# Layer 1 of a four-layer graph network: the message pass also folds weights and makes the node's part of the update; update, norm and layer 2's tables run on by groups

## The chip, the cores and the metric

The kernel runs on one core of a Trainium2 chip. The metric is the device time in microseconds (us), the median of the runs of one kernel. Engines are named as the profile names them: PE (TensorE products, PEld its weight loads), DVE (VectorE), ACT (ScalarE), POOL (GpSimd), SP (SyncE, which here issues DMAs).

## What is computed

A graph of 6250 nodes with 128 features and 106250 edges (self loops included) goes through four layers. Each layer takes `h = relu(layernorm(x))` and adds its result to `x`. Layer 0 is a hypergraph attention, layer 3 two graph attentions. The change lies in layer 1, a message network, and at the beginning of layer 2, a gated edge network:

```python
# layer 1, x is h
msg_in = concatenate([x[row], x[col]], axis=-1)
h = relu(msg_in @ mW1 + mb1)
messages = h @ mW2 + mb2
aggregated = segment_sum(messages, col, num_segments=N)
upd_in = concatenate([x, aggregated], axis=-1)
g = relu(upd_in @ uW1 + ub1)
return relu(g @ uW2 + ub2)
# layer 2, what is a function of the node alone
src_h = feat @ W_src + b_src
dst_h = feat @ W_dst + b_dst
se, de = src_h[edge_src], dst_h[edge_dst]
h = gelu(se @ W1a + de @ W1b + b1)
gate = sigmoid(gelu(se @ Wg1a + de @ Wg1b + bg1) @ Wg2 + bg2)
```

The product with `mW2` is linear, so the kernel sums the edges' `h` first and multiplies per node: `aggregated = (sum of h) @ mW2 + degree * mb2`. Likewise `W_src @ [W1a | Wg1a]` and `W_dst @ [W1b | Wg1b]` are folded on the chip, and layer 2's edges gather ready rows from a table of the source's part, while the target's part stays in SBUF.

## The kernel before

The nodes are 49 blocks of 128; `GROUPS` puts them into 12 groups of four blocks and a last one of one block. The edges, sorted by target, make 232 groups of 4 x 128. A stage that goes over nodes is a loop over `t`, in which `staged(t, s)` gives stage `s` the group `t - s`. Everything is ordered by hand: one instruction list for each of five engines, semaphores between them, and `meet()`, at which all five wait for each other, between stages.

**Layer 1's pass** (`c_po`, `c_ve`, `c_ac`, `c_sp`, `c_pe`, one body per edge group). GpSimd gathers the edges' rows by four indirect DMAs into a ring of eight (L619). PE spreads the values of two target blocks over the edges by one-hot matrices, in three bf16 products (L1258); VectorE adds the gathered rows (L1210), ScalarE takes the relu (L1226), PE sums the edges by target, 129 columns wide so that the last is the degree (`sum_pe`, L981), into one of four PSUM banks (`AGc`), and VectorE adds the two sums to `ACC` (`add_ve`, L966 and L969). SP loads the one-hot matrices.

**The update** (`u_pe`, `u_ac`, `u_ve`) has six stages, for each group: turn the sums in `ACC` (`turn4`, L1717) and copy them out on ScalarE; multiply by `mW2` (`times`, L1730), and on VectorE degree times `mb2` (L2085) plus that product (L2088); turn `H` (the node's h) and that result, and copy both out; multiply by the two halves of `uW1`, add `ub1` (L2094), relu on ScalarE; turn, copy out; multiply by `uW2`, add `ub2` (L2099), relu (L2076), add to `X` (L2101). Each of its PSUM tiles has one bank; of each working tile in SBUF there are two.

**The norm** (`stats_ve`, `stats_po`, `scale_ve`, `norm_ac`) goes in four parts of 13, 12, 12 and 12 blocks: VectorE takes mean and variance (L547, L550, L554), GpSimd the power -1/2 (L566), VectorE the product with the mean (L560), ScalarE writes `H = relu(X * rs - mean * rs)` block by block (L581).

**Layer 2's beginning** (`l2_sp`, `l2_pe`, `l2_ac`, `l2_ve`): SP loads 19 weights (L2127) and spills `X` to DRAM; VectorE clears `ACC`; PE folds the weights (four products); then for each group PE turns `H`, ScalarE copies it out (L2173), PE multiplies by both folded weights of 256 columns, and VectorE adds the biases (L2193, L2195); SP stores the source's part as the table (L2131). At the end SP loads `Wg2` (L2135) and waits for it. After a meeting layer 2's pass begins with its gathers (L619).

## Time and profile before

| | |
|---|---|
| median of 3 runs (lowest, highest) | 11647.88 us (11646.78, 11650.18) |
| profiled execution, span | 11656.4 us |
| PE busy | 7944.2 us (68%) |
| DVE busy | 7999.2 us (69%) |
| ACT busy | 5679.0 us (49%) |
| POOL busy | 7499.3 us (64%) |

These are sums over a span with many stages, so they don't tell what binds one. The stages around the change, in us from the span's start: layer 1's pass 6188.9 to 7354.1, its last additions to 7361.0; the update to 7434.5; the norm to 7460.9; folding of layer 2's weights to 7477.4; its tables to 7526.2; the first gather of layer 2's pass at 7530.2. In the views, "x" is a count, a releaser behind "<-" is what ended the wait ahead of an instruction, and the granted clock is a share of TensorE's full speed (1.00 is 2.4 GHz, 0.50 is 1.2 GHz). A matmul's duration contains time in PE's pipeline, so successive ones overlap; how long a run of products keeps the queue is the distance between starts.

### The profile page before, as it was taken

What the parts mean: (1) busy time and instruction counts of PE and PEld (TensorE: products, weight loads), DVE (VectorE), ACT (ScalarE), POOL (GpSimd) and SP (SyncE); (2) the same over time, 40 slices, a digit from 0 to 9 for tenths busy, and PEclk for the clock granted to TensorE, in tenths of its full rate; (3) what the DMA queues carried; (4) which work ended last, traced back from release to release, by engine and by line L of the source; (5) the groups of instructions that cost most, each with busy time, mean ns of one, the idle gap of its engine ahead of it and who ended that gap; (6) DMA issues with size and microseconds to landing.
All of it is one profiled execution on the core that took longest, in us unless ns stands there. A gap on an engine that the chain in (4) does not pass through costs nothing. (4 is left out here: it accounts for less than half of the span.)

```text
span 11656.4 us, 187371 instructions
## 1 busy us (share of the span) xinstructions
PE 7944.2 (68%) x47022; PEld 5850.1 (50%) x47022; DVE 7999.2 (69%) x33310; ACT 5679.0 (49%) x17077; POOL 7499.3 (64%) x7673
## 2 busy tenths in 40 slices
...
GB/s 17 9 20 51 55 55 55 73 122 120 120 121 65 55 55 55 90 216 214 215 163 116 132 131 131 91 155 154 154 153 107 132 140 137 138 106 137 139 137 114
DMA packets 712781, 1297.42 MB, mean 111 GB/s; under 512 B 196562, under 2 KB 369072, under 8 KB 711216
## 3 DMA queue, kind: packets, MB, share of 16 engines
...
q1 hardware_dynamic: 388992, 615.05, 16.5%
...
## 5 line engine op out<-in xcount | busy, mean ns | idle before, releaser
L619 POOL DMA_INDIRECT WK<-tab,IDX x4640 | 4408.7, 950 | 1833.5 <-issue 1335.3
L1522 POOL DMA_INDIRECT B<-tab,IDX x1856 | 1782.1, 960 | 765.6 <-issue 531.9
L619 POOL DMA_INDIRECT H<-tab,IDX x928 | 880.2, 948 | 577.3 <-DVE H L1327 263.3
L1541 DVE TENSOR_REDUCE WK<-PS 128x4 f32<-128x1024 f32 x928 | 1131.1, 1220 | 127.4 <-PE PS L1667 122.3
L1652 ACT ACTIVATE B<-B 128x33 f32<-128x33 f32 x5568 | 1210.7, 308 | 7.9
L922 PE MATMUL PS<-B 128*128 128x130 f32 (+1 forms) x3712 | 777.5, 374 | 393.4 <-ACT B L895 393.2
L1700 PEld LDWEIGHTS PS<-B,H 128*128 128x128 f32 x3712 | 829.8, 333 | 377.8 <-issue 372.4
L1700 PE MATMUL PS<-B,H 128*128 128x132 f32 x3712 | 893.9, 435 | 177.9 <-DVE ACC L1554 177.9
L1667 PE MATMUL PS<-WK,B 27*128 27x512 bf16 x1856 | 689.7, 481 | 389.6 <-DVE WK L1541 386.0
L922 PEld LDWEIGHTS PS<-B 128*128 128x128 f32 x3712 | 661.7, 268 | 581.5 <-ACT B L895 581.5
L883 ACT ACTIVATE B<-PS,PICK 18x512 bf16<-18x512 f32 x464 | 357.0, 769 | 1139.6 <-PE PS L940 1124.0
L981 PE MATMUL PS<-B,WK 128*128 128x129 f32 x1856 | 439.5, 410 | 612.8 <-ACT B L1018 612.8
L1210 DVE TENSOR_TENSOR WK<-PS,WK 128x512 f32<-128x512 f32 x232 | 160.5, 692 | 850.7 <-DMA WK<-tab,IDX 850.7
L459 POOL DMA_INDIRECT pieces<-WK,B x208 | 357.9, 1721 | 574.9 <-ACT WK L447 304.2
L981 PEld LDWEIGHTS PS<-B,WK 128*128 128x128 f32 x1856 | 371.9, 298 | 674.2 <-ACT B L1018 674.2
L1018 ACT ACTIVATE B<-WK 128x128 f32<-128x128 f32 x1856 | 588.3, 388 | 239.1 <-ACT B L694 96.1
L1226 ACT ACTIVATE WK<-WK 128x512 f32<-128x512 f32 x232 | 146.7, 632 | 1028.1 <-DVE WK L1210 1028.1
L1258 PE MATMUL PS<-B 128*128 x2784 | 310.0, 275 | 491.6 <-DVE WK L1210 482.4
L981 PE MATMUL PS<-B 128*128 128x129 f32 x1856 | 459.8, 425 | 257.2 <-ACT B L1018 256.9
L895 ACT ACTIVATE B<-WK 128x128 f32<-128x128 f32 x1856 | 584.6, 385 | 0.0
L966 DVE TENSOR_TENSOR ACC<-ACC,PS 128x129 f32 x928 | 260.2, 280 | 445.3 <-PE PS L981 422.1
L981 PEld LDWEIGHTS PS<-B 128*128 128x128 f32 x1856 | 395.2, 314 | 312.0 <-ACT B L1018 311.2
...
## 6 DMA issues: line engine op xcount, KB each, us to landing
H<-onehots SPq DMA_DIRECT2D x232, 768.0 KB
B<-onehots SPq DMA_DIRECT2D x232, 384.0 KB
onehots<-B ACTq DMA_DIRECT2D x232, 384.0 KB
...
onehots<-WK SPq DMA_DIRECT2D x232, 256.0 KB
B<-onehots SPq DMA_DIRECT2D x232, 256.0 KB
WK<-onehots SPq DMA_DIRECT2D x232, 256.0 KB
onehots<-B SPq DMA_DIRECT2D x232, 128.0 KB
```

The lines of the kernel that those rows point to most:

```text
L459: po.indirect_dma_start(out=recd[o], out_offset=bass.IndirectOffsetOnAxis(ap=ROWI[:, o, 2 * k + q:2 * k + q + 1], axis=0), in_=OUT[x % 4][ ...
L619: po.indirect_dma_start(out=G[:, g % n, k, :], out_offset=None, in_=table, in_offset=bass.IndirectOffsetOnAxis(ap=IDX[:, idx, t:t + 1], ax ...
L883: ac.activation(aETb[:, r % 2, :], PS[0:18, 2 + r % 2, :], ACT.Identity, bias=abi[0:18, :], scale=asc[0:18, :]).then_inc(S.n1, 1)
L895: i = ac.activation(aR[:, r % 2, k, 0:128], aG[:, g % 10, k, 0:128], ACT.Copy, scale=aEW[:, r % 2, k:k + 1])
L922: mm = pe.matmul(aAG(r, k // 2)[:, 0:n], aOH[:, g % 10, k, :], aR[:, r % 2, k, 0:n], start=k % 2 == 0, stop=k % 2 == 1)
L981: mm = pe.matmul(AG(r, k // 2), OH[:, r, k, :], R[:, r % n, k, 0:129], start=k % 2 == 0, stop=k % 2 == 1)
L1018: i = ac.activation(bR[:, r % 2, k, 0:128], bG[:, r, k, 0:128], ACT.Copy, scale=bEW[:, r % 2, k:k + 1])
L1522: po.indirect_dma_start(out=eG[:, g % 5, k, :], out_offset=None, in_=tab[TW3], in_offset=bass.IndirectOffsetOnAxis(ap=IDX[:, o, t:t + 1], ...
L1541: ve.tensor_reduce(eM2[:, g, b:b + 2, 2 * i:2 * i + 2, 1] if isinstance(g, int) else eM2[:, bass.ds(g, 1), b:b + 2, 2 * i:2 * i + 2, 1].re ...
L1652: i = ac.activation(eR[:, q, k, 33 * h:33 * h + 33], eG[:, g % 5, k, 33 * h:33 * h + 33], ACT.Copy, scale=eEX[:, r, 4 * k + h:4 * k + h + 1])
L1667: mm = pe.matmul(PS[:, b + h, :], eSEL[:, b + h, :], eET[:, r, 512 * i:512 * i + 512], start=True, stop=True)
L1700: mm = pe.matmul(eAG(k // 2), eSTo[:, r, k // 4, 128 * (k % 4):128 * (k % 4) + 128], eR[:, r % 2, k, 0:132], start=k % 2 == 0, stop=k % 2 ...
```

## The change

Of layer 1's weights, `mb2` is no longer loaded with the others. The message pass gets these steps beside its own:

- SP issues 21 loads, one with each of 21 edge groups from the fifth on: `mb2` as a column, layer 2's 19 weights, and `Wg2`.
- Around edge groups 32 to 45 (`FOLD2`) PE, ScalarE and VectorE fold weights: `mW2 @ uW1`'s lower half takes the place of `mW2`, `mb2 @ uW1`'s lower half that of `mb2`, and layer 2's products and biases are made.
- From edge group 48 on, every 14 groups (`ahead`), one of the 13 node groups of `H` is turned, copied out on ScalarE, multiplied by `uW1`'s upper half, and written back to `H` with `ub1` added.

The copies and products use PSUM banks 6 and 7, so the pass's sums have banks 4 and 5 alone (`AGc` by `r % 2`), and the sum of an edge group waits until the group two before it is added.

The update then needs, for each group: turn the sums, multiply by the folded weight, on VectorE degree times the folded bias plus the new `H` (four `scalar_tensor_tensor`, one per block) plus the product; turn, relu in ScalarE's copy; multiply by `uW2`; on VectorE add `ub2`, then relu and addition to `X` in one `scalar_tensor_tensor`. PSUM tiles are two banks each. Between update, norm and tables there is no meeting any more. Statistics and scaling of a part stand in `u_ve` behind the group that completes it, and `NORM5` puts pieces of ScalarE's norm between its copies; `l2_pe` waits for the part that it needs. GpSimd clears `ACC` (`l2_po`). The spill of `X` waits for the last addition. The other changed lines count one meeting fewer.

VectorE, a round inside the update, before (`WK` and `WT` are working and weight areas of SBUF, `PS` is PSUM):

```order
L2085 TENSOR_TENSOR WK<-ACC,WT 128x512
L2088 TENSOR_TENSOR WK<-WK,PS 128x512
L2094 TENSOR_TENSOR WK<-PS,WT 128x512
L2099 TENSOR_TENSOR WK<-PS,WT 128x512
L2101 TENSOR_TENSOR X<-X,WK 128x512
```

and now, a round before which a part of `X` was completed:

```order
L547 BN_STATS WK<-X 128x6 x12
L550 BN_AGGR WK<-WK 128x2 x12
L554 TENSOR_SCALAR WK<-WK 128x12
L2152 SCALAR_TENSOR_TENSOR WK<-WT,ACC,H 128x128 x4
L2156 TENSOR_TENSOR WK<-WK,PS 128x512
L2163 TENSOR_TENSOR WK<-PS,WT 128x512
L2164 SCALAR_TENSOR_TENSOR X<-WK,X 128x512
L560 SCALAR_TENSOR_TENSOR WK<-WK 128x12
```

The statistics, which stood behind the last addition, have moved between the rounds, and one round stands between a part's statistics and its scaling.

PE, a round inside the update, before:

```order
L1717 MATMUL PS<-ident,ACC 128x128 x4
L1730 MATMUL PS<-WT,WK 128x128 x4
L1717 MATMUL PS<-ident,H 128x128 x4
L1717 MATMUL PS<-ident,WK 128x128 x4
L1730 MATMUL PS<-WT,WK 128x128 x8
L1717 MATMUL PS<-ident,WK 128x128 x4
L1730 MATMUL PS<-WT,WK 128x128 x4
```

and now, the last rounds of the update and the first products of the tables:

```order
L1803 MATMUL PS<-ident,WK 128x128 x4
L1816 MATMUL PS<-WT,WK 128x128 x4
L1803 MATMUL PS<-ident,WK 128x128
L1816 MATMUL PS<-WT,WK 128x128 x5
L1803 MATMUL PS<-ident,H 128x128 x8
L1816 MATMUL PS<-LOW,WK 128x256 x8
```

The turning of `H` and the product with it have left the round, and the tables' transpositions follow the last update product directly (`LOW` is the area that now holds the folded weights).

ScalarE, from the update's end to the tables, before:

```order
L2072 ACTIVATE WK<-PS 128x128
L2076 ACTIVATE WK<-WK 128x512
L2076 ACTIVATE WK<-WK 128x128
L581 ACTIVATE H<-X,WK 128x128 x49
L2168 ACTIVATE WK<-PS 128x128 x2
L2173 ACTIVATE WK<-PS 128x512 x12
L2173 ACTIVATE WK<-PS 128x128
```

and now:

```order
L2134 ACTIVATE WK<-PS 128x512
L2139 ACTIVATE H<-X,WK 128x128 x4
L2134 ACTIVATE WK<-PS 128x128
L2139 ACTIVATE H<-X,WK 128x128 x24
L2219 ACTIVATE WK<-PS 128x512 x12
L2219 ACTIVATE WK<-PS 128x128
```

The run of 49 norms is in pieces between the update's copies; 24 of them stand behind the last one.

The diff, cut to its core:

```diff
-AGc = lambda r, k: PS[:, 4 + r % 4, 256 * k:256 * k + 129]
+AGc = lambda r, k: PS[:, 4 + r % 2, 256 * k:256 * k + 129]
...
+FOLD2 = (32, 36, 40, 42, 45)
...
+def ahead(j, lag):
...
+    i, rest = divmod(j - lag - 48, 14)
+    return (i, *GROUPS[i]) if rest == 0 and 0 <= i < NGR else None
...
@@ -1211,6 +1234,26 @@
...
+        if j == FOLD2[0]:
+            ve.wait_ge(s_w2, 16 * 21)
+            own(ve, "ve", ve.tensor_scalar(bg2, bg2, 0.5, None, ALU.mult))
+            ve.tensor_copy(mb2, mbc.broadcast_to([128, 128]))
+            ve.tensor_copy(cFB[0], bsd[:, 0:1].broadcast_to([128, 128]))
+            ve.tensor_copy(cFB[1], bsd[:, 1:2].broadcast_to([128, 128])).then_inc(s_fb, 1)
+        if j == FOLD2[2]:
+            ve.wait_ge(s_fp, 1)
+            ve.tensor_copy(w2, PS[:, 7, 0:128])
+            ve.tensor_copy(mb2, PS[:, 7, 128:256])
+            ve.tensor_copy(Wsd[0], PS[:, 7, 256:512])
+            ve.tensor_copy(Wsd[1], PS[:, 6, 0:256])
+            ve.tensor_copy(bsr[0], PS[:, 6, 256:512]).then_inc(s_fc, 1)
+        if j == FOLD2[4]:
+            ve.wait_ge(s_fp, 2)
+            ve.tensor_tensor(bsr[1], PS[:, 6, 0:256], b1g, ALU.add).then_inc(s_fc, 1)
+        if f := ahead(j, 6):
+            i, b0, n = f
+            ve.wait_ge(s_hq, i + 1)
+            ve.tensor_tensor(H[:, b0:b0 + n, :], slim(7, n), rep(ub1, n), ALU.add).then_inc(s_hu, 1)
...
+        if j == FOLD2[0]:
+            ac.wait_ge(s_ft, 1)
+            ac.activation(cFT, PS[:, 6, 0:384], ACT.Copy).then_inc(s_ftc, 1)
+        if f := ahead(j, 0):
+            i, b0, n = f
+            ac.wait_ge(s_hc, i + 1)
+            ac.activation(cHT[:, 0:128 * n], PS[:, 6, 0:128 * n], ACT.Copy).then_inc(s_hch, 1)
...
     for j in range(NG + 6):
+        if 4 <= j < 25:
+            d_, v = loads[j - 4]
+            sp.dma_start(d_, v, allow_slow_non_contiguous=True).then_inc(s_w2, 16)
...
-            sum_pe(pe, at, g, r % 4, cSTo, cR, AGc, 4, 4)
+            sum_pe(pe, at, g, r % 4, cSTo, cR, AGc, 2, 4)
...
+        if j == FOLD2[0]:
+            pe.wait_ge(s_w2, 16 * 21)
+            pe.transpose(PS[:, 6, 0:128], w2, ident[:, :])
+            for i in range(2):
+                t = pe.transpose(PS[:, 6, 128 + 128 * i:256 + 128 * i], raw[i], ident[:, :])
+            t.then_inc(s_ft, 1)
+        if j == FOLD2[1]:
+            pe.wait_ge(s_ftc, 1)
+            pe.wait_ge(s_fb, 1)
+            pe.matmul(PS[:, 7, 0:128], cFT[:, 0:128], u1[:, 128:256], start=True, stop=True)
+            pe.matmul(PS[:, 7, 128:256], mb2, u1[:, 128:256], start=True, stop=True)
+            pe.matmul(PS[:, 7, 256:512], cFT[:, 128:256], lowf[:, 256:512], start=True, stop=True)
+            pe.matmul(PS[:, 6, 0:256], cFT[:, 256:384], lowf[:, 512:768], start=True, stop=True)
+            pe.matmul(PS[:, 6, 256:512], cFB[0], lowf[:, 256:512], start=True, stop=True).then_inc(s_fp, 1)
+        if j == FOLD2[3]:
+            pe.wait_ge(s_fc, 1)
+            pe.matmul(PS[:, 6, 0:256], cFB[1], lowf[:, 512:768], start=True, stop=True).then_inc(s_fp, 1)
+        if f := ahead(j, 0):
+            i, b0, n = f
+            if i == 0:
+                pe.wait_ge(s_fc, 2)
+            else:
+                pe.wait_ge(s_hch, i)
+            turn4(pe, 6, lambda k: H[:, b0 + k, :], n).then_inc(s_hc, 1)
+        if f := ahead(j, 3):
+            i, b0, n = f
+            pe.wait_ge(s_hch, i + 1)
+            if i >= 1:
+                pe.wait_ge(s_hu, i)
+            times(pe, slim(7, n), n, [(cHT, u1[:, 0:128])]).then_inc(s_hq, 1)
...
-    for d_, n in ((mb1, "mb1"), (mb2, "mb2"), (ub1, "ub1"), (ub2, "ub2")):
+    for d_, n in ((mb1, "mb1"), (ub1, "ub1"), (ub2, "ub2")):
...
+NORM5 = {8: (0, 0, 5), 9: (0, 5, 9), 10: (0, 9, 13), 11: (1, 0, 4), 12: (1, 4, 8), 13: (1, 8, 12),
+         14: (2, 0, 4), 15: (2, 4, 8), 16: (2, 8, 12), 17: (3, 0, 12)}
...
 def u_pe(pe):
...
+    for t in range(NGR + 3):
...
+            if i >= 2:
+                pe.wait_ge(s_uah, i - 1)
+            turn4(pe, i % 2, lambda k: ACC[:, b0 + k, 0:128], n).then_inc(s_ua, 1)
...
+            if i >= 2:
+                pe.wait_ge(s_um, i - 1)
+            times(pe, slim(2 + i % 2, n), n, [(uAH[i % 2], w2)]).then_inc(s_up, 1)
...
-            if i >= 1:
-                pe.wait_ge(s_uch, i)
-            turn4(pe, 3, lambda k: H[:, b0 + k, :], n).then_inc(s_uc, 1)
             pe.wait_ge(s_um, i + 1)
...
+            if i >= 2:
+                pe.wait_ge(s_ubh, i - 1)
+            turn4(pe, 4 + i % 2, lambda k: by128(uZ[i % 2])[:, k, :], n).then_inc(s_ub, 1)
...
             i, b0, n = f
...
             pe.wait_ge(s_ubh, i + 1)
...
-            times(pe, slim(4, n), n, [(uCH[i % 2], u1[:, 0:128]), (uBH[i % 2], u1[:, 128:256])]).then_inc(s_uq, 1)
...
+            if i >= 2:
+                pe.wait_ge(s_ux, i - 1)
+            times(pe, slim(6 + i % 2, n), n, [(uDH[i % 2], u2)]).then_inc(s_ur, 1)
...
 def u_ac(ac):
...
+    for t in range(NGR + 5):
...
-            ac.wait_ge(s_uc, i + 1)
+            ac.wait_ge(s_ub, i + 1)
...
-            ac.activation(uCH[i % 2][:, 0:128 * n], PS[:, 3, 0:128 * n], ACT.Copy).then_inc(s_uch, 1)
-            ac.wait_ge(s_ub, i + 1)
-            ac.activation(uBH[i % 2][:, 0:128 * n], PS[:, 2, 0:128 * n], ACT.Copy).then_inc(s_ubh, 1)
+                ac.wait_ge(s_ur, i - 1)
+            ac.activation(uDH[i % 2][:, 0:128 * n], PS[:, 4 + i % 2, 0:128 * n], ACT.Relu).then_inc(s_ubh, 1)
+        if t in NORM5:
+            q, lo, hi = NORM5[t]
+            ac.wait_ge(s_scale, part_no(5, q))
+            for b in range(PARTS[q][0] + lo, PARTS[q][0] + hi):
+                last = ac.activation(H[:, b, :], X[:, b, :], ACT.Relu, bias=NMN[:, b:b + 1], scale=RSN[:, b:b + 1])
+            if PARTS[q][0] + hi == PARTS[q][1]:
+                last.then_inc(s_np, 1)
...
+def u_ve(ve):
+
+    for t in range(NGR + 3):
+        if f := staged(t, 1):
+            i, b0, n = f
+            Z = by128(uZ[i % 2])[:, 0:n, :]
+            if i >= 2:
+                ve.wait_ge(s_ub, i - 1)
+            for k in range(n):
+                last = ve.scalar_tensor_tensor(Z[:, k, :], mb2, ACC[:, b0 + k, 128:129], H[:, b0 + k, :],
+                                               ALU.mult, ALU.add)
+            own(ve, "ve", last)
+            ve.wait_ge(s_up, i + 1)
+            ve.tensor_tensor(Z, Z, slim(2 + i % 2, n), ALU.add).then_inc(s_um, 1)
...
+            F = by128(uF)[:, 0:n, :]
+            if i >= 1:
+                ve.wait_ge(s_ux, i)
+            ve.wait_ge(s_ur, i + 1)
+            own(ve, "ve", ve.tensor_tensor(F, slim(6 + i % 2, n), rep(ub2, n), ALU.add))
+            last = ve.scalar_tensor_tensor(X[:, b0:b0 + n, :], F, 0.0, X[:, b0:b0 + n, :], ALU.max, ALU.add)
+            last.then_inc(s_ux, 1)
+            if i in (3, 6, 9, 12):
+                ve.wait_ge(s_ux, i + 1)
+                stats_ve(ve, X, 5, i // 3 - 1)
+            if i in (4, 7, 10):
+                scale_ve(ve, 5, i // 3 - 1)
+    scale_ve(ve, 5, 3)
...
 def l2_sp(sp):
...
-        sp.dma_start(d_, v, allow_slow_non_contiguous=True).then_inc(s_w2, 16)
+    sp.wait_ge(s_ux, NGR)
     sp.dma_start(xs, flat(X[:, :, :])).then_inc(s_xs, 16)
...
     sp.wait_ge(s_xs, 16)
-    sp.dma_start(dWG, bcast(g2("Wg2").rearrange("p o -> (p o)"), 128)).then_inc(s_wg, 16)
-    sp.wait_ge(s_wg, 16)
+
+def l2_po(po):
+    po.wait_ge(s_um, NGR)
+    po.memset(flat(ACC[:, :, :]), 0.0)
...
 def l2_pe(pe):
...
     for t in range(NGR + 1):
         if f := staged(t, 0):
             i, b0, n = f
+            pe.wait_ge(s_np, next(q for q in range(4) if b0 + n <= PARTS[q][1]) + 1)
...
-            pe.wait_ge(s_fc, 1)
...
 def l2_ac(ac):
-    for i in range(2):
-        ac.wait_ge(s_ft, i + 1)
-        ac.activation(tmp[i], PS[:, 7 - 5 * i, 0:128], ACT.Copy).then_inc(s_ftc, 1)
+
     for i, (b0, n) in enumerate(GROUPS):
...
 def l2_ve(ve):
-    ve.memset(flat(ACC[:, :, :]), 0.0)
-    ve.wait_ge(s_w2, 16 * 19)
-    ve.tensor_scalar(bg2, bg2, 0.5, None, ALU.mult)
-    for i in range(2):
-        ve.tensor_copy(tmp[2 + i], bsd[:, i:i + 1].broadcast_to([128, 128])).then_inc(s_fb, 1)
-    for i in range(2):
-        ve.wait_ge(s_fp, 2 * i + 1)
-        ve.tensor_copy(Wsd[i], PS[:, 5 + i, 0:256])
-        ve.wait_ge(s_fp, 2 * i + 2)
-        last = ve.tensor_copy(bsr[i], PS[:, 3 + i, 0:256])
-    own(ve, "ve", last)
-    ve.tensor_tensor(bsr[1], bsr[1], b1g, ALU.add).then_inc(s_fc, 1)
-    ve.wait_ge(s_fc, 1)
+
     for i, (b0, n) in enumerate(GROUPS):
...
     stats_po(po, 5)
-    meet(po)
+    l2_po(po)
...
     meet(ve)
     u_ve(ve)
-    norm_ve(ve, 5)
-    meet(ve)
     l2_ve(ve)
```

## Rows read from the trace of the kernel before

**Rows 1.** Stretches: window; length; busy of PE, PEld, DVE, ACT, POOL; clock; DMA share, GB/s.

```profile
6188.90:7354.10 1165.20, 671.16 (x4632) 593.79 (x4632) 275.49 (x685) 146.05 (x231) 882.64 (x928) 0.70 0.46 131
7361.10:7434.50 73.40, 68.67 (x588) 67.22 (x588) 41.59 (x66) 40.56 (x78) 0.00 (x0) 0.96 0.00 1
7434.50:7460.90 26.40, 0.00 (x0) 0.00 (x0) 14.31 (x107) 18.94 (x49) 9.24 (x4) 0.51 0.00 1
7477.40:7526.20 48.80, 47.31 (x237) 41.10 (x237) 30.16 (x26) 6.65 (x12) 0.00 (x0) 1.00 0.40 136
```

**Rows 2.** Timeline of PE, one update round: start, duration, operation, [idle before, releaser].

```profile
7391.62 0.60 PE L1717 MATMUL PS<-ident,WK 128*128 128x128 f32 x4
7392.06 1.06 PE L1730 MATMUL PS<-WT,WK 128*128 128x128 f32 x8
7392.95 0.60 PE L1717 MATMUL PS<-ident,ACC 128*128 128x128 f32 x4
...
7396.94 0.60 PE L1717 MATMUL PS<-ident,WK 128*128 128x128 f32 x4
```

**Rows 3.** Timeline of ScalarE, the norm.

```profile
7441.90 18.94 ACT L581 ACTIVATE H<-X,WK 128x128 f32<-128x128 f32 x49 [7.76 <-DVE WK L560]
```

**Rows 4.** Timeline of SP's queue and GpSimd, the end of the tables.

```profile
7527.10 0.35 SPq L2135 DMA_DIRECT2D X<-in_L_gnn_Wg  x1
...
7530.22 1.02 POOL L619 DMA_INDIRECT H<-tab,IDX  x1 [78.99 <-SPq L152]
```

**Rows 5.** Timeline of PE, layer 1's start.

```profile
6145.14 3.44 PE L1730 MATMUL PS<-WT,WK 128*128 128x256 f32 x8 [4.86 <-DMA WT<-in_L_gnn_ub]
```

**Rows 6.** Timeline of PE, the update's start.

```profile
7363.88 1.91 PE L1730 MATMUL PS<-WT,WK 128*128 128x128 f32 x8
7365.59 1.06 PE L1717 MATMUL PS<-ident,ACC 128*128 128x128 f32 x4
7366.73 1.13 PE L1730 MATMUL PS<-WT,WK 128*128 128x128 f32 x8
```

**Rows 7.** Timeline of PE and VectorE, the end of layer 1's pass.

```profile
7357.06 2.06 PE L981 MATMUL PS<-WK,B 128*128 128x129 f32 x8 [2.94 <-ACT WK L1226]
...
7360.72 0.29 DVE L969 TENSOR_TENSOR ACC<-ACC,PS 128x129 f32 x1
```

**Rows 8.** Timeline of PE, the end of layer 2's pass.

```profile
8956.16 2.06 PE L981 MATMUL PS<-WK 128*128 128x129 f32 x8 [1.02 <-DVE ACC L969]
```

**Rows 9.** Timeline of VectorE, the end of layer 0.

```profile
6062.53 3.23 DVE L1884 SCALAR_TENSOR_TENSOR ACC<-ACC,WK,WT 128x128 f32<-128x128 f32 x12
```

**Rows 10.** Timeline of VectorE, the update.

```profile
7394.54 0.69 DVE L2101 TENSOR_TENSOR X<-X,WK 128x512 f32<-128x512 f32 x1 [0.70 <-ACT WK L2076]
7395.15 0.68 DVE L2085 TENSOR_TENSOR WK<-ACC,WT 128x512 f32<-128x512 f32 x1
7395.87 0.69 DVE L2088 TENSOR_TENSOR WK<-WK,PS 128x512 f32<-128x512 f32 x1
```

**Rows 11.** Timeline of GpSimd, the powers at layer 0's end.

```profile
6069.44 2.38 POOL L566 TENSOR_TENSOR WK<-WK 128x12 f32<-128x12 f32 x1 [4.22 <-DVE WK L554]
6076.27 3.92 POOL L566 TENSOR_TENSOR WK<-WK 128x12 f32<-128x12 f32 x1 [4.44 <-DVE WK L554]
```

**Rows 12.** Groups of GpSimd by form: busy, mean ns, idle before.

```profile
L262 POOL MEMSET B<- 128x128 f32 x1 | 0.2, 204 | 0.0
```

**Rows 13.** Stretches, as in rows 1, after layer 2's pass.

```profile
8990.00:9000.00 10.00, 4.67 (x38) 4.10 (x38) 9.56 (x15) 1.79 (x3) 0.00 (x0) 1.00 0.00 0
```

**Rows 14.** One source line: lowest, median and highest ns, when, form.

```profile
L299 DVE SCALAR_TENSOR_TENSOR B<-B x2: 1026/1026/1026, 10.5 to 15.4; 128x832 f32<-128x832 f32 x2
```

**Rows 15.** Timeline of PE and VectorE inside layer 1's pass.

```profile
6834.06 0.69 DVE L1210 TENSOR_TENSOR WK<-PS,WK 128x512 f32<-128x512 f32 x1 [4.30 <-DMA WK<-tab,IDX]
...
6835.00 1.65 PE L1258 MATMUL PS<-B 128*128 x12 [2.29 <-DVE WK L1210]
6835.09 0.29 DVE L969 TENSOR_TENSOR ACC<-ACC,PS 128x129 f32 x1
```

More of the change, by code:

```diff
@@ L1190, in build @@
         cSTo = room(fcs, 4, 4, 128)
-        AGc = lambda r, k: PS[:, 4 + r % 4, 256 * k:256 * k + 129]
+        AGc = lambda r, k: PS[:, 4 + r % 2, 256 * k:256 * k + 129]
         SQP = B2[:, 0:NB * 192].bitcast(BF16)
+        cHT = room(fc, 512)
+        lowf, wgtf = LOW[:, :, :].rearrange("p o t -> p (o t)"), WGT[:, :, :].rearrange("p o t -> p (o t)")
+        raw = [lowf[:, 128 * i:128 * i + 128] for i in range(6)]
+        Wsd = [lowf[:, 768 + 256 * i:1024 + 256 * i] for i in range(2)]
+        bsr = [lowf[:, 1280 + 256 * i:1536 + 256 * i] for i in range(2)]
+        b1g = wgtf[:, 0:256]
+        cFT = wgtf[:, 256:640]
+        cFB = [wgtf[:, 640 + 128 * i:768 + 128 * i] for i in range(2)]
+        bsd, mbc = wgtf[:, 1796:1798], wgtf[:, 1798:1799]
+        W2, W3, Wo = (wgtf[:, 900 + 128 * i:1028 + 128 * i] for i in range(3))
+        b3b, gb, bb, bob = (wgtf[:, 1284 + 128 * i:1412 + 128 * i] for i in range(4))
+        b2c, bg2 = wgtf[:, 1799:1800], wgtf[:, 1800:1801]
+        dWG = IDX[:, 2, 0:128].bitcast(F32)
+        s_w2 = sem("w2")
+        s_ft, s_ftc, s_fp, s_fc, s_fb = sem("fold_t"), sem("fold_tc"), sem("fold_p"), sem("fold_c"), sem("fold_b")
+        s_hc, s_hch, s_hq, s_hu = (sem("hu_" + n) for n in ("turned", "copied", "product", "ready"))
+        FOLD2 = (32, 36, 40, 42, 45)
+        g2 = lambda n: a["L2_gnn_" + n]
+        def ahead(j, lag):
+            i, rest = divmod(j - lag - 48, 14)
+            return (i, *GROUPS[i]) if rest == 0 and 0 <= i < NGR else None
         def c_po(po, p):
```

134 lines of the change are left out of this document (23 added, 111 removed).

## The prediction

> **What bounds the kernel now.** I first read the table of stretches around the update [rows 1]: the message pass, the update, norm, and layer 2's tables, with the folding of layer 2's weights between the last two (7460.9 to 7477.4, 16.5 us). What to see is which engine fills each. The pass fills none of TensorE, VectorE or ScalarE; GpSimd's gathers do: 928 in 1165.2 us, one every 1.256, so a group of four every 5.02 us. The update is 73.4 us with PE busy for 68.7 at nearly full clock [rows 1]. A round of it on PE [rows 2]: four transpositions take 0.44 us of the queue, eight passes of products 0.89, and the round comes back after 5.32 us; that is four transpositions and four sets of products for a group. VectorE idles for almost half of it. Then PE stops. In the norm VectorE works 14.3 of 26.4 us [rows 1], and ScalarE scales all 49 blocks in one run of 18.94 us once the first part of the statistics is through [rows 3]. In the folding everybody waits for 19 weights that are asked for only then. The tables are bound by PE, 47.3 of 48.8 us [rows 1]. Last, SP issues one more load at 7527.10, and the first gather of layer 2's pass starts at 7530.22 [rows 4].
>
> From the update's first transposition to that gather these stages are serial, and no other stage runs beside them: what they lose in length, the kernel loses.
>
> **Layer 1's start.** One load of eight (mb2) goes away. The first product waits for the last load, ub2, to 6145.14 [rows 5]; a load is issued about every half microsecond. I take -0.5 us (0 to -0.5).
>
> **The pass.** It gets 21 loads on SP, a folding of some 15 instructions, and for each of 13 groups four transpositions, four products, a copy on ScalarE and an addition on VectorE. At low clock eight passes take 1.91 us [rows 6], so this is 1.0 and 1.9 us of PE in two turns of 5.02 us; PE is busy 671 of 1165 us here [rows 1], so 2.1 us of a turn are free. The gathers set the pace and are issued up to eight groups ahead. I take 0 for the body of the pass. If that cover were gone, the 13 groups would cost some 13 x 2.9 = 38 us.
>
> The products need two PSUM banks, so the pass's sums have two in place of four: the sum of group g now waits until group g-2 is added, before until g-4 was. Behind that wait on PE's queue stand the products for the next groups' edges, and VectorE waits for those. With the ring of gathers in between this shifts PE by a turn; it shows at the end. When the last rows have landed, before only the last sum was left (PE at 7357.06), and VectorE's last addition began at 7360.72 [rows 7]. Now three sums are left, two more at 2.06 us, with additions in between; one of the two lies beside additions that were there before. +2.2 us. The bounds are 0 and 6.2: the latter is twice the 3.08 us a group of layer 2's pass, which has one such bank, and where PE waits 1.02 us for an addition between sums of 2.06 [rows 8].
>
> **The update.** PE keeps, for a full group, two sets of transpositions and two of products: 2 x (0.44 + 0.89) = 2.66 us at full clock in place of 5.32 [rows 2]. VectorE's list for a group is now four scalar_tensor_tensor of 128 columns, two additions with an input from PSUM, and a scalar_tensor_tensor of 512. Twelve of the first kind take 3.23 us, 0.27 each [rows 9]; an addition of 512 columns takes 0.61 of the queue, and 0.72 where the next one waits for its result [rows 10]; I take the last kind for the same. So 4 x 0.27 + 0.11 + 0.61 + 0.72 + 0.61 = 3.13 us: VectorE, not PE, becomes the bound. For 49 blocks that is 12.25 x 3.13 = 38.3 us. Three of four parts of the statistics now stand inside the loop: 14.3 x 37/49 = 10.8 us. Before a part can be scaled, GpSimd takes a power: 2.38 us beside scalar_tensor_tensors of 128 columns, 3.92 beside long additions of two SBUF tensors [rows 11]. VectorE has 3.13 us of other work between, most of it of the first kind or from PSUM: no wait for the first, 0.8 us a part for the second. I take 0 for three parts (0 to 2.4). The start: PE begins at half speed [rows 6], and the first group has to pass both transpositions and both products before VectorE's second half begins, some 9.2 us in, of which VectorE can use 5.4; 3.8 us are lost. Sum: 38.3 + 10.8 + 3.8 = 52.9 in place of 73.4, so -20.5 us. The lower bound is 51 (a quicker start); the upper is rival 1's 69.
>
> By the Trainium skill (SBUF — State Buffer, Who interferes with whom) a VectorE instruction with two SBUF inputs and a GpSimd instruction that reads SBUF contend for one read interface, whatever the length. By that rule all three powers would take the 3.92, and the sum would be 2.4 us larger; the row of 2.38 beside instructions with two SBUF inputs speaks against it for short ones.
>
> **From update to tables.** Before, 42.9 us lie between the last X and the first table product (7434.5 to 7477.4) [rows 1]. Now 37 of 49 blocks are normalized beside the update: ScalarE has 1.2 us of copies a round and 1.6 of norms (4 x 18.94/49), less than VectorE's 3.13. The weights are ready. What stays behind the last X is one chain: statistics of twelve blocks 3.5 us (14.3 x 12/49), power 2.4 with its hand-over, scaling 0.2, twelve norms on ScalarE 12 x 0.387 = 4.7, and ScalarE's copy of the first transposed group 0.7, which stands behind the norms in its queue. 11.5 us: -31.4 us. Bounds: 9 and 14, with a power of 3.9 and ScalarE still at norms of the third part. The clearing of ACC goes from VectorE to GpSimd; a memset of 128 columns takes 204 ns there [rows 12], so 6517 need 5 to 11 us, and the tables hide it until the next gather, some 50 us later; if they didn't, it would cost those 5 to 11. The spill of X moves behind the update; SP has nothing else until the first table is ready.
>
> **The tables** don't change: 48.8 us. But before them PE now stands idle for some 11 us, where before the folding had brought its clock up. At such a start eight passes took 1.91 us, and 1.13 three microseconds later [rows 6]. I add 2.2 us (0 to 4).
>
> **The end.** The last load (Wg2) is gone. Of the 3.1 us between its issue and the gather [rows 4] some 0.3 stays for the meeting: -2.8 us (-3.1 to 0).
>
> Sum: -0.5 + 0 + 2.2 - 20.5 - 31.4 + 2.2 - 2.8 = -50.8 us. It is made in the profiled execution, whose span is 11656.4; the median of the runs is 11647.9, 8.5 lower (0.07%). Taken from the median: 11597.
>
> **Order.** The three pairs of listings in the section on the change show what this rests on: on VectorE the statistics stand between rounds, on PE a round loses two transpositions and two products and runs on into the tables, and on ScalarE the run of 49 norms becomes pieces, with 24 at the end.
>
> **Rivals.** (1) PE stays the bound of the update at its lower clock: it is no longer full, and the statistics leave gaps. In the pass it is busy 58% at a mean clock of 0.70 [rows 1]. At half speed eight passes keep the queue for 1.71 us [rows 6], 0.214 each; 49 blocks of six passes are 63 us, with the start 69: +16, 11613. Against it: behind layer 2's pass the same kind of loop keeps clock 1.00 with PE busy 4.67 of 10 us [rows 13]. 0.11.
>
> (2) ScalarE's pieces of norm stand in one queue with the copies that PE waits for. If each piece held up a round, the 14.2 us of norms taken out of the chain (18.94 - 4.7) would come back: 11611. Against it: a round needs 2.8 us of ScalarE and 3.1 of VectorE, and PE makes a product up to three rounds before VectorE wants it. 0.09.
>
> (3) The new scalar_tensor_tensor of 512 columns runs at half rate: 0.53 us more in each of 12.25 rounds, +6.5, 11603. The row of such an instruction with two f32 SBUF inputs says no: 832 columns took 1026 ns [rows 14]. 0.05. The Trainium skill (Vector Engine (DVE) Microarchitecture Reference, 7. Points that are easy to get wrong) says that this shape with two SBUF sources that are not bf16 halves its throughput; the trace here disagrees.
>
> (4) Slower: the pass loses its slack to the two banks. If each group waited for the one before it through VectorE's three additions, the sum and the edge products, a turn would be 1.32 + 2.06 + 1.65 [rows 8, 15] and three hand-overs of 0.14, 5.4 us in place of 5.02: 232 x 0.4, some +90, so 11687. It decides from 0.22 us a turn (50.8/232). Against it: the chain runs from group g to g+3, and has three turns' time. 0.06.
>
> (5) The edit does less than it says: (1) and (2) together, +30, 11627. 0.04.
>
> **Numbers.** Forecast 11597, chance 0.65 (its own range 11588 to 11607); the rivals as given. A measurement here can tell about 0.2%, 23 us, from no change. Faster by more: forecast and (1) to (3), 0.90; within: (5), 0.04; slower: (4), 0.06. The range reaches from the forecast's low bounds over (3), (2) and (1), with 8 us for their own spread: 11588 to 11621. (4) and (5) are left out, 0.10, and some of the rest.
>
> **What would show it.** Right: gathers of the pass still 1.256 us apart; an update of 51 to 55 us with VectorE busy for nine tenths; 11 to 12 us from the last X to the first table product, with ScalarE in norms near the end; tables of 51; the gather within 1.5 us behind them. Wrong: turns of the pass over 5.1 us; PE full at clock 0.5 in the update; VectorE's additions in the update waiting for PE in every round; a scalar_tensor_tensor of 512 columns over 0.75 us; gathers that wait for the memset.

## The result and the profile after

| | median | lowest, highest | runs |
|---|---|---|---|
| before | 11647.33 us | 11635.98, 11650.18 | 4 |
| changed | 11584.98 us | 11576.71, 11590.38 | 4 |

The ratio is 0.9948, with a 95% interval of 0.9933 to 0.9962: faster by 62 us, where 51 were forecast, and 3 us below the range's low end (11588). The interval reaches from -78 to -44 us, so it holds the forecast.

The stretches of the changed kernel, in the columns of [rows 1]: the pass up to its last gather, its end, the update, the last X to the first table product, the tables.

```profile
6175.57:7340.80 1165.23, 665.72 (x4778) 605.39 (x4778) 285.21 (x708) 153.00 (x245) 882.76 (x928) 0.71 0.44 132
7340.80:7349.14 8.34, 4.40 (x24) 4.24 (x24) 3.50 (x11) 0.63 (x1) 0.00 (x0) 0.63 0.03 8
7349.24:7402.25 53.01, 39.27 (x302) 37.67 (x302) 48.89 (x169) 26.31 (x57) 7.04 (x3) 0.90 0.00 1
7402.25:7413.69 11.44, 0.00 (x0) 0.00 (x0) 3.67 (x27) 7.69 (x21) 7.74 (x2) 0.62 0.66 281
7413.69:7464.79 51.10, 49.75 (x237) 42.75 (x237) 30.15 (x26) 6.68 (x12) 0.00 (x0) 0.95 0.36 124
```

The update's row shows the bound that has moved: VectorE 48.89 of 53.01 us (92%), PE 39.27. In the row behind it PE does nothing for 11.44 us. Set beside the prediction's terms, by the starts and ends in the two traces:

| term | forecast | measured | from |
|---|---|---|---|
| layer 1's start | -0.5 | -0.1 | 146.9 to 146.8 us, last gather of the pass before it to first gather of this one |
| body of the pass | 0 | +0.1 | 1164.2 to 1164.3 us, first to last gather |
| end of the pass | +2.2 | +1.4 | 7.9 to 9.3 us, last gather's start to last addition's end |
| update | -20.5 | -20.4 | 73.4 to 53.0 |
| last X to first table product | -31.4 | -31.5 | 42.9 to 11.4 |
| tables | +2.2 | +2.3 | 48.8 to 51.1 |
| tables' end to the next gather | -2.8 | -2.7 | 4.0 to 1.3 |
| sum | -50.8 | -50.9 | |

The spans of these two executions differ by 67.7 us (11656.4 to 11588.7). So 17 us fell away in places where the two programs do the same.

They fell away at the very beginning: the first gather of layer 0's first pass starts at 1033.72 us before and at 1013.88 after. Ahead of it the edges are sorted, by 208 indirect gathers of GpSimd, one after the other (L459). The groups of that line before and after (busy, mean ns | idle ahead of it, releasers):

```profile
L459 POOL DMA_INDIRECT pieces<-WK,B x208 | 357.9, 1721 | 574.9 <-ACT WK L447 304.2 <-DMA pieces<-WK,B 264.6 <-issue 6.1
```

```profile
L459 POOL DMA_INDIRECT pieces<-WK,B x208 | 357.3, 1718 | 557.0 <-ACT WK L447 290.7 <-DMA pieces<-WK,B 257.9 <-issue 8.4
```

The gathers' own time is the same; the idle time ahead of them, some 2 us each besides the wait ahead of the first, is 17.9 us shorter. Is that the change's doing (it could be, by another placement of code or data), or does this stage take a different time in each execution? That is what the first experiments ask.

### The profile page after: what moved, and what is told of

Same layout as the page of the kernel before. It is cut to its first block and busy times, and to the rows that moved or that the text cites. A ratio compares the mean times of both kernels' runs of the same rounds, so it can differ in the third digit from the quotient of the medians.

```text
span 11588.7 us, 187063 instructions
## 1 busy us (share of the span) xinstructions
PE 7905.0 (68%) x46880; PEld 5826.0 (50%) x46880; DVE 7996.7 (69%) x33347; ACT 5661.9 (49%) x17037; POOL 7507.3 (65%) x7674
## 5 line engine op out<-in xcount | busy, mean ns | idle before, releaser
L922 PEld LDWEIGHTS PS<-B 128*128 128x128 f32 x3712 | 667.3, 269 | 581.6 <-ACT B L895 581.6
L981 PE MATMUL PS<-WK,B 128*128 128x129 f32 x1856 | 386.7, 374 | 496.9 <-ACT WK L1269 350.6
L459 POOL DMA_INDIRECT pieces<-WK,B x208 | 357.3, 1718 | 557.0 <-ACT WK L447 290.7
L981 PEld LDWEIGHTS PS<-WK,B 128*128 128x128 f32 x1856 | 334.2, 270 | 543.9 <-issue 542.5
```

The lines of the kernel that those rows point to most:

```text
L459: po.indirect_dma_start(out=recd[o], out_offset=bass.IndirectOffsetOnAxis(ap=ROWI[:, o, 2 * k + q:2 * k + q + 1], axis=0), in_=OUT[x % 4][ ...
L922: mm = pe.matmul(aAG(r, k // 2)[:, 0:n], aOH[:, g % 10, k, :], aR[:, r % 2, k, 0:n], start=k % 2 == 0, stop=k % 2 == 1)
L981: mm = pe.matmul(AG(r, k // 2), OH[:, r, k, :], R[:, r % n, k, 0:129], start=k % 2 == 0, stop=k % 2 == 1)
```

## Experiments

The quantity read in each profile is the time from the start of the last gather of layer 1's pass to the first gather of layer 2's, called the touched stretch: 177.1 us before, 126.2 in the changed kernel. It repeats to within a microsecond, where whole executions of one kernel differ by twenty and more.

**Before against itself, and the changed kernel again.** Both kernels unchanged.

> The kernel before, unchanged, timed against itself. Theory A (the change acts only in the stages it touches, where the two profiles differ by -51 us; the rest of the measured -62 is scatter of stages that it leaves alone): ratio 1.000 within 0.1%, and the sorting stage at the start (first to last of its 208 gathers), 824.9 us in the profile of before and 806.5 in that of after, takes some other value here between 800 and 830. Theory B (the change shortens that stage too, in every execution): ratio 1.000 as well, but the sorting stage near 825 again.

Measured: ratio 1.0003 (0.9994 to 1.0013); sorting stage 815.5 us; touched stretch 177.7.

> The changed kernel, unchanged, timed once more in five rounds. Theory A: -51 us, a ratio of 0.9956 (0.9950 to 0.9962), with the sorting stage anywhere from 800 to 830 us and the span from the pass's last gather to layer 2's first gather again 126 us (177 before). Theory B: -62 to -67 us, a ratio of 0.9943 to 0.9947, with the sorting stage near 806 again.

Measured: 11597.48 us against 11656.24 (-58.8), ratio 0.9950 (0.9936 to 0.9963); sorting stage 829.3 us, touched stretch 126.1. Of these four profiles the sorting stage is longest in the kernel for which theory B wants it short. A third comparison, on another occasion:

> The changed kernel, unchanged, timed a third time: in two comparisons the medians lay 62 and 59 us below before, while the stages that the change touches lost 51.0 and 51.6 us in the profiles (before against null_before and the changed kernel twice), and what lies outside them ranged over 11462 to 11487 us in ten profiles whatever the kernel. Theory A (scatter of the sorting stage): the three comparisons scatter around -51, so this one may come out between -42 and -60. Theory B' (some 8 to 10 us more fall away in executions without a profile, outside the touched stages): again -59 to -62.

Measured: 11602.10 against 11650.83 (-48.7), ratio 0.9956 (0.9942 to 0.9969); sorting stage 822.1, touched stretch 126.7. With the other profiles (their kernels follow below), each split into the sorting stage (start of the first to start of the last of its 208 gathers), the touched stretch and everything else:

| kernel | span | sorting stage | touched stretch | the rest |
|---|---|---|---|---|
| before | 11656.4 | 824.9 | 177.1 | 10654.4 |
| null_before | 11646.8 | 815.5 | 177.7 | 10653.6 |
| two_banks | 11664.4 | 828.3 | 179.6 | 10656.5 |
| fold_early | 11644.6 | 820.8 | 163.0 | 10660.8 |
| changed | 11588.7 | 806.5 | 126.2 | 10655.9 |
| null_after | 11609.0 | 829.3 | 126.1 | 10653.6 |
| null_after_b | 11600.4 | 822.1 | 126.7 | 10651.5 |
| norms_apart | 11606.1 | 823.4 | 129.3 | 10653.4 |
| no_ahead | 11613.6 | 828.6 | 132.3 | 10652.7 |
| one_bank | 11620.3 | 834.2 | 133.7 | 10652.4 |
| tables_early | 11595.4 | 825.5 | 113.7 | 10656.2 |
| tables_early_b | 11573.2 | 808.2 | 113.7 | 10651.2 |

The rest stays within 10 us in all twelve; the sorting stage takes 806 to 834 us, within one and the same kernel too (806, 829, 822 in the changed one). Theory B falls: the change does nothing to that stage. Its longest case, in the group of the same line (one_bank):

```profile
L459 POOL DMA_INDIRECT pieces<-WK,B x208 | 359.7, 1729 | 581.8 <-ACT WK L447 327.4 <-DMA pieces<-WK,B 244.4 <-issue 10.1
```

Here the waits are 6.9 us longer than before and the gathers 1.8. Nor does the chip decide it: on each of the three chips on which the ten later profiles were taken, the stage differs from one execution to the next (815.5 to 829.3 us, 820.8 to 834.2, and 808.2 against 822.1).

Three comparisons gave -62, -59 and -49 us by their medians, and -61, -56 and -51 by the means of the same runs, with standard errors of 4, 6 and 3. The third lies within theory A's range and outside that of theory B', though these means alone do not exclude a few us beyond the 51. Eleven of the twelve profiles (all but the first of before) are of executions among the timed runs, and each time is some 1.7 us above its span, so for these the table shows what the time is made of. That the other timed runs scatter by this stage too is inferred, since a run without a profile shows no stages.

**Two banks alone.** In the kernel before:

```diff
-AGc = lambda r, k: PS[:, 4 + r % 4, 256 * k:256 * k + 129]
+AGc = lambda r, k: PS[:, 4 + r % 2, 256 * k:256 * k + 129]
-    sum_pe(pe, at, g, r % 4, cSTo, cR, AGc, 4, 4)
+    sum_pe(pe, at, g, r % 4, cSTo, cR, AGc, 2, 4)
```

> The kernel before with two PSUM banks in place of four for the sums of layer 1's pass, and nothing else. By my term: the gathers keep their 1.256 us, and the time from the last gather's start to the end of the last addition goes from 7.9 us to some 10 (the changed kernel shows 9.3). By rival 4 of the prediction: turns of 5.4 us in place of 5.02, the pass some 90 us longer.

Measured: 1165.5 us from first to last gather (1164.2 and 1165.6 in the two profiles of before), so the body keeps its pace, and 10.1 us from the last gather to the last addition. PE's last sums (timeline):

```profile
7357.88 2.06 PE L981 MATMUL PS<-WK,B 128*128 128x129 f32 x8 [2.86 <-ACT WK L1226]
7362.86 5.35 PE L981 MATMUL PS<-WK,B 128*128 128x129 f32 x24 [2.92 <-ACT WK L1226]
```

Three sums in one row (24 products of 129 columns), where [rows 7] has one of 8: the term is as it was derived. In the changed kernel's first profile the same row took less:

```profile
7343.83 4.40 PE L981 MATMUL PS<-WK,B 128*128 128x129 f32 x24 [3.03 <-ACT WK L1269]
```

In null_after it took 5.50 us. Over the nine executions with two banks the end takes 9.2 to 10.4 us, so the +1.4 of the first profile is one value out of +1.3 to +2.5. Rival 4 falls here.

**One bank.** In the changed kernel:

```diff
-AGc = lambda r, k: PS[:, 4 + r % 2, 256 * k:256 * k + 129]
+AGc = lambda r, k: PS[:, 4, 256 * k:256 * k + 129]
-    sum_pe(pe, at, g, r % 4, cSTo, cR, AGc, 2, 4)
+    sum_pe(pe, at, g, r % 4, cSTo, cR, AGc, 1, 4)
```

> The changed kernel with one PSUM bank in place of two for the pass's sums: each sum waits for the additions of the group before. By my term the body keeps its pace (a chain of sum and additions takes 3.1 us as in layer 2's pass, a turn 5.02) and the end grows: from the last gather to the last addition 12 to 14 us (9.3 with two banks, 7.9 with four). By rival 4 of the prediction a turn would now be 5.4 us or more: the gathers of the pass, 1164 us, take 1250.

Measured: 1164.2 us from first to last gather, so even one bank costs the body nothing. The end took 16.7 us, beyond my 12 to 14. PE there:

```profile
7365.90 2.06 PE L981 MATMUL PS<-WK,B 128*128 128x129 f32 x8 [3.59 <-ACT WK L1269]
...
7368.98 2.06 PE L981 MATMUL PS<-WK,B 128*128 128x129 f32 x8 [1.02 <-DVE ACC L969]
...
7372.05 2.06 PE L981 MATMUL PS<-WK,B 128*128 128x129 f32 x8 [1.01 <-DVE ACC L969]
...
7375.12 2.06 PE L981 MATMUL PS<-WK,B 128*128 128x129 f32 x8 [1.02 <-DVE ACC L969]
```

Four sums are left behind the last rows, not three, each 3.07 us after the one before: one bank holds back one group more, and no sum lies beside an addition any longer. I had counted two extra sums as with two banks.

**The folding alone.** Update, norm and meetings as before, while GpSimd still clears `ACC`. Against the changed kernel the pass loses the steps for `mW2`, `mb2` and `H`:

```diff
 if j == FOLD2[0]:
-    ve.tensor_copy(mb2, mbc.broadcast_to([128, 128]))
...
 if j == FOLD2[2]:
-    ve.tensor_copy(w2, PS[:, 7, 0:128])
-    ve.tensor_copy(mb2, PS[:, 7, 128:256])
     ve.tensor_copy(Wsd[0], PS[:, 7, 256:512])
...
-if f := ahead(j, 0):
...
 u_ve(ve)
+norm_ve(ve, 5)
+meet(ve)
 l2_ve(ve)
```

> One part of the change alone: layer 2's weights (and Wg2) are loaded and folded inside layer 1's pass, whose sums get two banks for it; update, norm and the meetings are those of the kernel before. Read from the start of the pass's last gather to layer 2's first gather: 177.1 us before, 126.2 in the changed kernel. By my terms: -16.5 for the folding, -2.7 for Wg2, +2.2 for the banks, +2.3 because PE then comes to the tables idle as in the changed kernel: 162.4 (160 to 165). Rival: the folding had hidden something else (the clearing of ACC, the spill of X) that now becomes late: 170 or more.

Measured: 163.0 us, 0.6 from the sum. PE comes to the tables after a long idle time, as the row says, and turns its first two groups in 1.97 us:

```profile
7466.15 1.97 PE L1775 MATMUL PS<-ident,H 128*128 128x128 f32 x8 [28.12 <-ACTq L152]
```

So loading and folding early, `Wg2` with it, brings 14 us net of the banks and the clock.

**The norm apart.** In the changed kernel:

```diff
-if i in (3, 6, 9, 12):
-    ve.wait_ge(s_ux, i + 1)
-    stats_ve(ve, X, 5, i // 3 - 1)
-if i in (4, 7, 10):
-    scale_ve(ve, 5, i // 3 - 1)
...
-scale_ve(ve, 5, 3)
+ve.wait_ge(s_ux, NGR)
+norm_ve(ve, 5)
...
-if t in NORM5:
...
+for q in range(4):
+    scaled_ac(ac, H, X, ACT.Relu, 5, q).then_inc(s_np, 1)
```

> The changed kernel without its interleaved norm: statistics, powers, scaling and norms follow the update in the order of before (still without a meeting). By my terms: the update loses 10.8 us of statistics (53 to 42), and from the last X to the first table product come some 27.4 us (7.8 to the first norm, 18.9 of norms, 0.7 copy) in place of 11.4, so +5.2, 131.4 us from the pass's last gather to layer 2's first. Rival: the interleaving is worth the 14.2 us of norms that it takes out of the chain, 140.

Measured: 129.3 us, so the interleaving is worth 3.1, less than my 5.2 and far from the rival's 14. The update without the statistics (a window as in [rows 1], which leaves out the last 0.3 us), and PE from the update's end on:

```profile
7359.92:7399.90 39.98, 35.03 (x294) 32.91 (x294) 37.44 (x87) 14.67 (x26) 0.00 (x0) 1.00 0.01 1
```

```profile
7427.15 6.41 PE L1816 MATMUL PS<-LOW,WK 128*128 128x256 f32 x16 [12.35 <-ACT WK L2210]
```

The chain behind the update is as long as forecast (27 us from the last X to this row), but the update needs only 40.4 us (to 7400.24) in place of the 42.1 that the prediction counts without statistics, at a clock of 1.00. Inside the changed kernel's update the statistics cost 12.6 us, not the 10.8 that they take on VectorE. The rows on PE there say why:

```profile
7367.54 1.06 PE L1816 MATMUL PS<-WT,WK 128*128 128x128 f32 x8
7372.67 1.11 PE L1803 MATMUL PS<-ident,WK 128*128 128x128 f32 x4 [4.08 <-DVE WK L2156]
7373.58 1.92 PE L1816 MATMUL PS<-WT,WK 128*128 128x128 f32 x8
```

While VectorE takes statistics PE runs out of work for 4.08 us and starts again at half speed (1.92 for the eight products that took 1.06, at a granted clock of 0.51 until 7377.76). Behind two of the three sets VectorE then waits, for PE and for the last power:

```profile
7379.36 0.69 DVE L2163 TENSOR_TENSOR WK<-PS,WT 128x512 f32<-128x512 f32 x1 [0.46 <-PE PS L1816]
...
7399.75 0.17 DVE L560 SCALAR_TENSOR_TENSOR WK<-WK 128x12 f32<-128x12 f32 x1 [0.51 <-POOL WK L566]
7400.18 0.69 DVE L2163 TENSOR_TENSOR WK<-PS,WT 128x512 f32<-128x512 f32 x1 [0.26 <-PE PS L1816]
```

That is 1.2 of the 1.8 us.

**The node's part back in the update.** The steps of `ahead` are taken out of the pass; in the changed kernel's update:

```diff
-turn4(pe, i % 2, lambda k: ACC[:, b0 + k, 0:128], n).then_inc(s_ua, 1)
+turn4(pe, 0, lambda k: ACC[:, b0 + k, 0:128], n).then_inc(s_ua, 1)
...
+turn4(pe, 1, lambda k: H[:, b0 + k, :], n).then_inc(s_hc, 1)
...
-times(pe, slim(2 + i % 2, n), n, [(uAH[i % 2], w2)]).then_inc(s_up, 1)
+times(pe, slim(2 + i % 2, n), n, [(uCH[i % 2], u1[:, 0:128]), (uAH[i % 2], w2)]).then_inc(s_up, 1)
...
+ac.activation(uCH[i % 2][:, 0:128 * n], PS[:, 1, 0:128 * n], ACT.Copy).then_inc(s_hch, 1)
```

VectorE adds `ub1` where it added the ready `H`, and the turned sums have one PSUM bank in place of two.

> The changed kernel without the node's part in the pass: the update turns H, copies it out and multiplies it again, into the same PSUM tile as the sums' product; VectorE's list is the same as in the changed kernel (ub1 in place of the ready H). PE then has 4.0 us a round in place of 2.66, against VectorE's 3.13 and 10.8 of statistics. If VectorE is the bound and PE works through its statistics, 12.25 x 4.0 = 49 is still no more than VectorE's 49.1: 126 to 129 us from the pass's last gather to layer 2's first, so this part is worth 0 to 3 us. Rival: the statistics and PE's longer rounds add up (buffers too few): +10.6, 137.

Measured: 132.3 us, +6.1, between the two: neither holds as it stands. PE and VectorE in a round:

```profile
7386.26 1.95 PE L1795 MATMUL PS<-WT,WK 128*128 128x128 f32 x16
...
7390.24 0.94 PE L1795 MATMUL PS<-WT,WK 128*128 128x128 f32 x7
```

```profile
7385.65 0.69 DVE L2149 TENSOR_TENSOR WK<-PS,WT 128x512 f32<-128x512 f32 x1 [0.64 <-PE PS L1795]
...
7389.64 0.69 DVE L2149 TENSOR_TENSOR WK<-PS,WT 128x512 f32<-128x512 f32 x1 [0.64 <-PE PS L1795]
```

A round comes back after 3.98 us, PE is full, and VectorE waits for it. During statistics PE works on, but not to their end: in the whole update it waits for VectorE's L2142 four times, 0.56, 0.78, 0.94 and 3.95 us, so 6.2 of the 10.8 us of statistics add up, most of it behind the last set. Behind the first round no wait of PE ended with a copy of ScalarE, so the single bank doesn't show. The node's part in the pass is worth 6 us.

**Tables before the last norms.** In the changed kernel ScalarE's copies for the tables go first:

```diff
-14: (2, 0, 4), 15: (2, 4, 8), 16: (2, 8, 12), 17: (3, 0, 12)}
+}
+LATE5 = {1: (2, 0, 6), 2: (2, 6, 12), 3: (3, 0, 4), 4: (3, 4, 8), 5: (3, 8, 12)}
...
 ac.activation(HT2[i % 2][:, 0:128 * n], PS[:, i % 2, 0:128 * n], ACT.Copy).then_inc(s_ht2, 1)
+if i in LATE5:
+    piece_ac(ac, *LATE5[i])
...
-scale_ve(ve, 5, 3)
...
+if i == 0:
+    scale_ve(ve, 5, 3)
```

(`piece_ac` is the loop over norms under `NORM5`; the fourth store buffer lies elsewhere, as it overlapped with the norm's factors.)

> The changed kernel, with ScalarE's first two copies for the tables ahead of the norms of the last two parts (which follow in pieces between the next copies), and VectorE's last scaling behind the first table additions. Theory: of the 11.4 us between the last X and the first table product some 10 fall away and PE enters the tables at its full clock, so -11 us against the changed kernel (-9 to -13), -62 against before if theory A holds, and 0.9947. Rival: VectorE's statistics of the last part (3.5 us) and the single PSUM buffers hold the second group, and the waits only move: -4 to -6.

> The version with the tables' first copies ahead of the norms, timed again beside the changed kernel on the same chip. In the profile its touched stages take 113.7 us in place of 126.2, but the two medians of the first call differed by 1 us only. Theory A: -12.4 us against the changed kernel, with a scatter of some 6 us for the difference of two medians, so -6 to -19. Rival: what the profile shows in these stages is given back elsewhere, 0 to -3 again.

Measured: a touched stretch of 113.7 us in both, -12.4 against the changed kernel. Against before the two comparisons give 11596.44 to 11656.24 (-59.8; ratio 0.9946, 0.9932 to 0.9959) and 11575.81 to 11650.83 (-75.0; 0.9940, 0.9927 to 0.9954); the changed kernel beside them had -58.8 and -48.7. So the gain in the medians was 1 and 26 us (6 and 20 by the means of the runs). The second lies outside the 6 to 19 that were expected, on the far side from the rival. Both are off by about what the sorting stage moves (825.5 and 808.2 us in the two profiles), and their mean is near the profile's 12.4. The rival falls by the table, in which the rest is no longer than elsewhere. PE, ScalarE and VectorE at the tables' start:

```profile
7418.37 0.29 DVE L2167 SCALAR_TENSOR_TENSOR X<-WK,X 128x128 f32<-128x128 f32 x1
7418.45 3.72 PE L1816 MATMUL PS<-LOW,WK 128*128 128x256 f32 x16
7418.65 0.60 ACT L2221 ACTIVATE WK<-PS 128x512 f32<-128x512 f32 x1 [0.25 <-PE PS L1803]
7418.69 2.42 DVE L547 BATCH_NORM_STATS2 WK<-X 128x6 f32<-128x128 f32 x12
...
7423.53 3.69 PE L1816 MATMUL PS<-LOW,WK 128*128 128x256 f32 x16 [0.92 <-DVE WK L2231]
```

The first table product starts beside the last X and at full speed (3.72 for 16 products, which took 6.13 in the changed kernel); of VectorE's statistics only 0.92 us show on PE. By the touched stretch, and by the mean of its two comparisons, this version beats both kernels.

## Why the prediction was right in its sum and wrong in its range

**The terms held**, though that their sum is right to 0.1 us is in part luck: between executions layer 1's start takes 146.4 to 149.1 us, the body of the pass 1164.2 to 1165.6, its end with two banks 9.2 to 10.4. The terms of the touched stretch alone add up to -50.3 us; the pairs of its two profiles before and three of the changed kernel give -50.3 to -51.6.

The gathers stayed 1.256 us apart, so the pass hid 13 turns of additional work, and VectorE became the bound of the update. Its round in the changed kernel (timeline of VectorE), with one set of statistics:

```profile
7357.61 1.14 DVE L2152 SCALAR_TENSOR_TENSOR WK<-WT,ACC,H 128x128 f32<-128x128 f32 x4
7358.78 0.69 DVE L2156 TENSOR_TENSOR WK<-WK,PS 128x512 f32<-128x512 f32 x1
7359.38 0.68 DVE L2163 TENSOR_TENSOR WK<-PS,WT 128x512 f32<-128x512 f32 x1
7360.10 0.69 DVE L2164 SCALAR_TENSOR_TENSOR X<-WK,X 128x512 f32<-128x512 f32 x1
7360.71 1.13 DVE L2152 SCALAR_TENSOR_TENSOR WK<-WT,ACC,H 128x128 f32<-128x128 f32 x4
...
7367.03 2.61 DVE L547 BATCH_NORM_STATS2 WK<-X 128x6 f32<-128x128 f32 x13
```

A round takes 3.10 us, against 3.13 by the rows of before. Two errors inside this term cancelled. The statistics cost 1.8 us more than their own duration, most of it the three waits shown with norms_apart. And the update without them came out 1.7 us shorter than counted, which is the term of the start: it let PE begin at half speed, with VectorE's second half 9.2 us in and 3.8 us lost. PE and VectorE in the changed kernel, whose first transposition starts at 7349.24:

```profile
7350.65 1.16 PE L1816 MATMUL PS<-WT,WK 128*128 128x128 f32 x8 [0.31 <-ACT WK L2128]
...
7356.27 0.69 DVE L2163 TENSOR_TENSOR WK<-PS,WT 128x512 f32<-128x512 f32 x1
```

The first eight products took 1.16 us, where [rows 6] has 1.91, and the second half began 7.0 us in, so some 1.6 us were lost. The granted clock was 1.00 from 7349.24 to the first statistics; just before, PE had the three sums in one row that two banks leave. In one_bank, where PE waits 1.0 us between the last sums, the clock was 0.50 in them, and the update did begin at half speed:

```profile
7380.02 2.06 PE L1816 MATMUL PS<-WT,WK 128*128 128x128 f32 x8
```

Its second half began 8.4 us in. So the end of the pass and the start of the update hang together, and the prediction had priced them apart.

**Behind the last X** the chain is the one described. ScalarE, then GpSimd:

```profile
7399.96 4.72 ACT L2139 ACTIVATE H<-X,WK 128x128 f32<-128x128 f32 x12 [1.30 <-DVE WK L560]
7408.44 4.72 ACT L2139 ACTIVATE H<-X,WK 128x128 f32<-128x128 f32 x12 [3.75 <-DVE WK L560]
7413.07 1.06 ACT L2219 ACTIVATE WK<-PS 128x512 f32<-128x512 f32 x2
```

```profile
7371.01 2.45 POOL L566 TENSOR_TENSOR WK<-WK 128x13 f32<-128x13 f32 x1 [30.21 <-DVE WK L554]
...
7397.43 2.29 POOL L566 TENSOR_TENSOR WK<-WK 128x12 f32<-128x12 f32 x1 [10.68 <-DVE WK L554]
7405.93 2.26 POOL L566 TENSOR_TENSOR WK<-WK 128x12 f32<-128x12 f32 x1 [6.21 <-DVE WK L554]
7408.14 5.53 POOL L2192 MEMSET ACC<- 128x6517 f32 x1
7466.06 1.02 POOL L619 DMA_INDIRECT H<-tab,IDX  x1 [52.39 <-SPq L152]
```

The norms of the last twelve blocks stand ahead of the copy that the tables need, though the first table groups need none of them. I had described this and priced it, and not seen that it is an order one can change: tables_early takes 12 us out of it. The clearing of `ACC` takes 5.53 us, far ahead of the next gather, as bounded (5 to 11).

**The tables** start at half speed after the 11 us without work:

```profile
7413.69 6.13 PE L1816 MATMUL PS<-LOW,WK 128*128 128x256 f32 x16 [11.75 <-ACT WK L2219]
...
7423.99 3.62 PE L1816 MATMUL PS<-LOW,WK 128*128 128x256 f32 x16
```

6.13 in place of 3.62 us is the term of 2.2 (2.5 by these rows; the stretch grew by 2.3). The granted clock was 0.62 from 7413.69 to 7420.10 and 1.00 behind. In tables_early, where PE comes straight from the update, the term isn't there.

**The rivals.** (1) did not come: the update ran at a clock of 0.90, and PE fell to half speed only behind statistics. (2) did not: inside the update PE waited for VectorE's statistics, and behind the first round neither PE nor VectorE waited for a copy of ScalarE. (3) did not: the `scalar_tensor_tensor` of 512 columns with two SBUF inputs (L2164) takes 0.69 us, the addition beside it (L2163) 0.68. The Trainium skill (Vector Engine (DVE) Microarchitecture Reference, 7. Points that are easy to get wrong) has it at half throughput; the measurement decides against it here. On the Trainium skill's other rule (SBUF — State Buffer, Who interferes with whom): the three powers inside the update took 2.45 (13 columns), 2.29 and 2.29 us beside VectorE instructions with two SBUF inputs, the last of them beside one of 512 columns (L2164 at 7398.56). The fourth, for which VectorE waited, took 2.26. So here too the row of 2.38 was the nearer one; 3.92 was not seen in the update. (4) fell with two_banks and one_bank, and (5) with (1) and (2).

**The step that failed** is the range: "from the forecast's low bounds over (3), (2) and (1), with 8 us for their own spread". The 8 us went to the upper end (11613 + 8). The low end of 11588 came from the low bounds of the terms alone, -59.9 us in sum, with nothing for stages that the change leaves as they are. The text had one sign of them, the 8.5 us between the profiled execution and the median, and took it as a fixed offset. It is not one: a time is some 1.7 us above its span wherever both are known, so the profiled execution of before (span 11656.4) was itself slower than each of the four timed ones. The sorting at the start takes 806 to 834 us from one execution to the next, and the median of four runs carries that with it. Where the expected 51 us went, then: all of them are in the profile, and some 10 us more in the first comparison came from elsewhere; the other two gave -59 and -49. A range for the measured median needed some 10 us more on each side, for this alone.

What makes the sorting stage differ stays open. Shown is where: over the twelve profiles the gathers' own time is 354 to 363 us and the idle time ahead of them 557 to 582. Nor do the profiles reach every run. If in the lowest of the changed kernel (11576.71 us) the touched stretch and the rest were as in this kernel's profiles, some 793 to 797 us are left for its sorting stage, less than any profile shows.
